# A fused layer on Trainium2: SyncE's DMA queue, in place of GpSimd's, copies q into its stacks

## Chip, cores and metric

One Trainium2 chip, one core of it. The metric is the device time of one execution in microseconds, smaller is better.

## What is computed

The reference is one transformer layer on four sequences (B = 4) of 512 rows and 512 columns, all in float32. Cut to its core:

```python
q = rotary(heads(x @ Wq + bq))        # 16 heads of 32
k = rotary(x @ Wk + bk)               # one key head, one value head
v = x @ Wv + bv
attn = softmax(q @ k.T / sqrt(32))
x = layernorm(x + (attn @ v) @ Wo + bo)
h = sigmoid(x @ quant(w1).T) * (x @ quant(w2).T)   # 1408 wide, weights in -1, 0, 1
x = layernorm(x + h @ quant(w3).T)
```

## The kernel before, in words

The program is written out by hand: each engine has its own list of instructions, and semaphores tie the lists together. The four sequences are called b = 0 to 3 here, as in the code.

**Attention in steps.** From b = 1 on, a sequence is 32 steps, k = 0 to 31. Step k takes head h = k // 2 and its pair i = k % 2: two of the four blocks of 128 query rows. In each step TensorE multiplies the stacked q with the stacked k (`score`, line 1355), VectorE takes the row minimum (`row_max`, line 1046), ScalarE takes two exponentials (`exps`, line 752) and the upper f16 half of p (`p_high`, line 760), VectorE takes the lower half (`p_low`, line 1053), and one DMA transpose on SyncE's queue (`turn`, line 477) turns p into `pt_sb`. The step with number k turns the pair k - 1. Four heads later `context` (line 1413) multiplies the turned p with v, for four heads at once; it stands in TensorE's list at steps 12, 20 and 29 and, for the last four heads, at step 2 of the next sequence. The table `BESIDE` says what else TensorE does in each step: projections of q and k, and all of the feed-forward part of the sequence before. `exps` waits until the pair four earlier is turned, since p has four slots. So `turn` has about three steps to land, except for the last pair of a sequence, which the context at step 2 wants.

**How q comes to its stack.** For a group g of four heads, ScalarE adds the bias (`unit`), GpSimd and VectorE rotate (`rotation`, lines 532 to 540, and `pairs`, line 925), ScalarE copies the result to `hi`, rounded for the matmul (`high_half`, line 682), and VectorE puts the rest into `lo` (`halves`, line 956). `hi` and `lo` are one buffer each of 128 rows (four heads of 32 rows). `stack(engine, b, h)` (lines 421 to 432) then issues four DMAs of 64 KB that put the rows of head h of `hi` and `lo` on the 128 partitions of one of four slots of `q_st`, so that one matmul adds up the products of the halves. It waits until the slot's last head (four before) is scored, until `hi` is written and, ahead of its third DMA, until `lo` is. Who waits for a stack: `score` of that head in step 2h, and `high_half` of the next group (steps 2, 10, 18 and 26 of ScalarE's list), since it writes over `hi`.

**The queues.** For b = 0 SyncE's queue issues the stacks. For b = 1 to 3 GpSimd's list does, in between its rotations, `inverse_std` (lines 561 to 568, for the layer norms), `add_bias` (line 573) and the rounding of weights. SyncE's list for b = 1 to 3 is the 96 `turn`s, with the loads of xT (line 459, at step 7, for the next sequence) and of x (line 463, at the end of step 12), and the stores of finished rows (line 470, at steps 1, 2, 3 and 5). Each list goes on in order: what stands behind a wait waits too. `q_slot` gives the slot and the semaphore of a head; before, the stacks of SyncE and those of GpSimd count on separate semaphores (`q_in` and `q_by_pool`).

Of the kernel before, what the change touches and what calls it, by code (L numbers as in the profile page):

```python
# [31 lines left out]
B, T, D, H, F = 4, 512, 512, 16, 1408  # L32
# [4 lines left out]
HPG = H // HG  # L37
# [17 lines left out]
QR = 4  # L55
SUMS = 4
PIECES = 4
FIRST_RING = 4
WARM = 10
UNITS = ["q0", "k", "q1", "q2", "q3"]  # L60

# [140 lines left out]
def unit_count(s, name):  # L202

    return s * len(UNITS) + UNITS.index(name)


def layer(nc, xT, x, wq, small, wo, b_rows, w1, w2, w3, table, out):
    with ExitStack() as ctx:
# [3 lines left out]
        def sem(name):  # L212
            return ctx.enter_context(nc.semaphore(name))
# [112 lines left out]
        hi_done = sem("hi_done")  # L326
        lo_done = sem("lo_done")
        q_in = [sem(f"q_in{n}") for n in range(QR)]
        q_by_pool = [sem(f"q_by_pool{n}") for n in range(QR)]
        scored = sem("scored")  # L330
        maxed = sem("maxed")
        expd = sem("expd")
# [34 lines left out]
        def filled(use, s, n=0):  # L367

            name = banks_of(use, s)[n]
            return wide[name][1], at(name, use, s)  # L370
# [28 lines left out]
        def h_of(s):  # L399


            return h_last if s == B - 1 else h_sb

        def first_bank(n):
            return (score_banks[0:3] + [b_ps[:, :]])[n % FIRST_RING]

# [7 lines left out]
        def q_slot(b, h):  # L414

            n = b * H + h
            if b == 0:
                return n % QR, q_in[n % QR], (n // QR + 1) * 16 * 4
            return n % QR, q_by_pool[n % QR], ((n - H) // QR + 1) * 16 * 4

        def stack(engine, b, h):

            n, name = b * H + h, f"q{h // HPG}"
            slot, stacked, _ = q_slot(b, h)
            if n >= QR:
                engine.wait_ge(scored, (n - QR + 1) * TT)
            engine.wait_ge(hi_done, unit_count(b, name) + 1)
            for r in (0, 2, 1, 3):
                half = (hi, lo)[r % 2]
                if r == 1:  # L430
                    engine.wait_ge(lo_done, unit_count(b, name) + 1)
                engine.dma_start(q_st[HD * r:HD * (r + 1), slot, :].bitcast(F32),  # L432
                                 half[HD * (h % HPG):HD * (h % HPG + 1), :].bitcast(F32)).then_inc(stacked, 16)
# [18 lines left out]
        @block.sync  # L452
        def _(sp):
            def load_xT(s):
                if s:
                    sp.wait_ge(*filled("q3", s - 1))
                for half in range(2):
                    cols = slice(half * DT * T // 2, (half + 1) * DT * T // 2)
                    sp.dma_start(xT_sb[:, :, :].rearrange("p k t -> p (k t)")[:, cols],
                                 xT[s, :, cols]).then_inc(xT_in[half], 16)  # L460

            def load_x(s):
                sp.dma_start(xb, x[s, :, :].rearrange("(t p) d -> p t d", p=P)).then_inc(x_in, 16)

            def store(s, t):
                if s < B - 1:
                    sp.wait_ge(normed, s * TT + t + 1)
                else:
                    sp.wait_ge(last_normed, t + 1)
                sp.dma_start(out[s, t * P:(t + 1) * P, :], h_of(s)[:, t, :]).then_inc(h_free[t], 16)  # L470

            def turn(b, h, i):

                n = pair_of(b, h, i) % PSLOTS
                sp.wait_ge(p_lo, pair_of(b, h, i) + 1)
                sp.wait_ge(ctx_filled, (b * H + h - PTR) // HPG + 1)
                sp.dma_start_transpose(
                    pt_half[:, (b * H + h) % PTR, i, :, :, :, :].rearrange("p s t k q -> p (s t k) q"),
                    p_half[n][:, :, :].rearrange("p s c -> p (s c)")).then_inc(turned[n], 16)

            load_xT(0)
            sp.wait_ge(xT_in[1], 16)
            sp.dma_start(wq_sb[:, :, P:], wq[:, P:].rearrange("(k p) n -> p k n", p=P)).then_inc(wq_in, 16)
            sp.dma_start(stage[0][:, 0:DT * F // 2], w1[:, 0:DT * F // 2]).then_inc(w_ffn[0], 16)
            for h in range(HPG):
                stack(sp, 0, h)
            sp.dma_start(stage[0][:, DT * F // 2:], w1[:, DT * F // 2:]).then_inc(w1_rest, 16)
            sp.dma_start(stage[1], w2).then_inc(w_ffn[1], 16)
            stack(sp, 0, HPG)
            sp.dma_start(wo_sb[:, :, :], wo.rearrange("(k p) n -> p k n", p=P)).then_inc(wo_in, 16)  # L490
            for h in range(HPG + 1, 3 * HPG):
                stack(sp, 0, h)
            load_xT(1)
            for h in range(3 * HPG, H):
                stack(sp, 0, h)
            sp.wait_ge(rounded, 2 * PIECES)
            load_x(0)
            sp.dma_start(stage[2], w3).then_inc(w_ffn[2], 16)
            for t in range(TT):
                sp.sem_inc(h_free[t], 16)  # L500
            for b in range(1, B):
                for k in range(H * PAIRS):
                    if k == 7 and b < B - 1:
                        load_xT(b + 1)
                    if k:
                        turn(b, *divmod(k - 1, PAIRS))
                    elif b > 1:
                        turn(b - 1, H - 1, 1)
                    if b > 1 and k in (1, 2, 3, 5):
                        store(b - 2, (1, 2, 3, 5).index(k))  # L510
                    if k == 12:
                        sp.wait_ge(h_ready, b * TT)
                        load_x(b)
            turn(B - 1, H - 1, 1)
            for t in range(TT):
                store(B - 2, t)
            for t in range(TT):
                store(B - 1, t)
            for t in range(TT):
                sp.wait_ge(h_free[t], (B + 1) * 16)  # L520

        @block.gpsimd
        def _(pool):
# [64 lines left out]
                round_weight(1, c)  # L588
            rotation(1, "q0")
            cosines(1, "k")  # L590
            stack(pool, 1, 0)
            add_bias(0, 0)
            add_bias(0, 1)
            sines(1, "k")
            add_bias(0, 2)
            add_bias(0, 3)
            for h in range(1, HPG - 1):
                stack(pool, 1, h)
            for b in range(1, B):
                stack(pool, b, 3)  # L600
                if b > 1:
                    inverse_std(b - 2, 1, 2)
                rotation(b, "q1")
                if b > 1:
                    inverse_std(b - 2, 1, 3)
                stack(pool, b, 4)
                stack(pool, b, 5)
                rotation(b, "q2")
                stack(pool, b, 6)
                inverse_std(b - 1, 0, 0)  # L610
                inverse_std(b - 1, 0, 1)
                if b == 1:
                    pool.wait_ge(thr_step, 2 * 3)
                    round_weight(2, 0, 0)
                stack(pool, b, 7)
                inverse_std(b - 1, 0, 2)
                inverse_std(b - 1, 0, 3)
                if b == 1:
                    round_weight(2, 2, 1)
                stack(pool, b, 8)  # L620
                stack(pool, b, 9)
                rotation(b, "q3")
                if b == 1:
                    stack(pool, b, 10)
                    stack(pool, b, 11)
                    round_weight(2, 1, 2)
                    round_weight(2, 3, 3)
                add_bias(b, 0)
                if b > 1:
                    stack(pool, b, 10)  # L630
                add_bias(b, 1)
                if b > 1:
                    stack(pool, b, 11)
                add_bias(b, 2)
                add_bias(b, 3)
                for h in range(12, H):
                    stack(pool, b, h)
                if b < B - 1:
                    rotation(b + 1, "q0")
                if b < B - 1:  # L640
                    inverse_std(b - 1, 1, 0)
                    stack(pool, b + 1, 0)
                    stack(pool, b + 1, 1)
                    inverse_std(b - 1, 1, 1)
                    rotation(b + 1, "k")
                    stack(pool, b + 1, 2)
            for norm in NORMS[NORMS.index((B - 2, 1, 0)):]:
                inverse_std(*norm)

# [575 lines left out]
        def _(pe):  # L1225
# [102 lines left out]
            def first_score(h, t):  # L1328
                n = h * TT + t
                pe.wait_ge(expd, max(n - FIRST_RING + 1, 0))  # L1330
                if n == FIRST_RING - 1:
                    pe.wait_ge(*unit_drained(0, "k"))
# [211 lines left out]
            pe.wait_ge(ones_set, 1)  # L1544
            for _ in range(WARM):
                pe.matmul(score_banks[0][:, 0:P], ones[:, :], ones[:, :], start=True, stop=True)
# [88 lines left out]
```

## Time and profile before

| | us |
|---|---|
| median of 3 runs | 600.63 (598.98 to 602.34) |
| the profiled execution | 601.29 |
| its span in the trace | 599.4 |
| TensorE busy in the span | 546.4 (91%) |
| VectorE busy | 476.7 (80%) |
| ScalarE busy | 420.6 (70%) |
| GpSimd busy | 299.7 (50%) |

Durations below are from the profiled execution; all times of the trace are counted from the start of its span. In its rows PE is TensorE's matmul, DVE VectorE, ACT ScalarE, POOL GpSimd and SP SyncE; "SPq" and "POOLq" are their instruction queues, which issue DMAs. The duration of a DMA row on SPq or POOL is the time in which the queue issues it; the time to landing is given apart, from the start of the issue until the data is there. "x96" is a count, "<-" in brackets names what ended an idle time, and L432 is line 432.

### The profile page before, as it was taken

The numbers are of one execution on the slowest core, as the hardware profiler recorded it, in microseconds if no ns is written. First come the engines' busy times: TensorE is split into PE (matmuls) and PEld (weight loads), VectorE is DVE, ScalarE is ACT, GpSimd is POOL, SyncE is SP. The second block draws the span as 40 slices with busy tenths as digits, with TensorE's granted clock in tenths as the row PEclk, the third lists the DMA queues.
The fourth block names the chain that finished last, engine by engine and source line by source line (L and its number), as shares of the span: only waits on it lengthen the run. The fifth ranks groups of instructions, "written<-read, shape, count | busy, mean of one in ns | idle before, by whom it ended". The sixth has DMA issues, their size and how long they took to land.

```text
span 599.4 us, 9184 instructions
## 1 busy us (share of the span) xinstructions
PE 546.4 (91%) x2984; PEld 274.5 (46%) x2984; DVE 476.7 (80%) x639; ACT 420.6 (70%) x857; POOL 299.7 (50%) x398
## 2 busy tenths in 40 slices
PE   9788889898788999999799999999699999989993
PEld 5454445544444444454444445355244444444441
DVE  3788978978998999889989899889989897445433
ACT  2657757779787988787898888678979896233300
POOL 2209796928897734868357335896553300211011
PEclk9779999999979999999999999999799999999997
DMA  8680418239989997999999988989999989000001
GB/s 311 187 310 10 132 41 293 71 65 181 212 147 210 167 181 145 176 193 203 214 199 192 187 163 154 181 187 184 175 217 177 170 177 190 37 0 37 1 0 70
DMA packets 217119, 92.12 MB, mean 154 GB/s; under 512 B 204400, under 2 KB 205552, under 8 KB 216560
## 3 DMA queue, kind: packets, MB, share of 16 engines
q1 hardware_dynamic: 209952, 77.61, 63.9%
q0 software_dynamic: 6144, 12.60, 10.2%
q10 hardware_dynamic: 976, 1.33, 0.6%
q8 instruction: 24, 0.39, 0.3%
q14 instruction: 23, 0.19, 0.1%
HBM read 20.20 MB, written 4.19 MB: 41 GB/s over the span
## 4 chain that ended last, share of the span: by engine, by line
PE 62%; DVE 13%; issue 8%; ACT 8%; DMA 5%; POOL 2%; SPq 1%; ACTq 0%; POOLq 0%; DVEq 0%
PE a_ps L1310 12%; PE b_ps L1310 7%; PE c_ps L1413 7%; PE s_ps L1323 6%; PE s_ps L1355 5%; PE e_ps L1310 5%; DVE p_all L1053 3%; PE b_ps L1323 3%; PE a_ps L1241 3%; DMA pt_sb<-p_all 3%; PE c_ps L1395 3%; ACT p_all L752 2%; PE a_ps L1323 2%; DVE sh_sb L1046 2%; PE s_ps L1366 2%
## 5 line engine op out<-in xcount | busy, mean ns | idle before, releaser
L752 ACT ACTIVATE p_all<-s_ps,sh_sb 128x512 f32<-128x512 f32 x192 | 129.9, 682 | 58.5 <-DVE sh_sb L1046 55.5
L1053 DVE SCALAR_TENSOR_TENSOR p_all<-p_all 128x1024 f16<-128x1024 f32 x96 | 128.6, 1340 | 4.6 <-ACT p_all L760 4.5
L1046 DVE TENSOR_REDUCE sh_sb<-s_ps 128x2 f32<-128x1024 f32 x96 | 116.6, 1215 | 17.2 <-PE s_ps L1355 17.2
L760 ACT ACTIVATE p_all<-p_all 128x1024 f16<-128x1024 f32 x96 | 101.7, 1059 | 2.0
L1310 PE MATMUL a_ps<-late,q 128*128 128x512 f16 x352 | 83.5, 380 | 4.6 <-ACT th L723 2.9
L1355 PE MATMUL s_ps<-k_st,q_st 128*128 128x512 f32 x192 | 79.5, 496 | 2.8 <-ACT p_all L752 1.6
L432 POOL DMA_DIRECT2D q_st<-hi x96 | 49.4, 517 | 59.3 <-PE s_ps L1355 31.4
L561 POOL TENSOR_SCALAR rstd<-mv 128x1 f32<-128x1 f32 x32 | 9.9, 308 | 132.9 <-DVE mv L1013 132.8
L1310 PEld LDWEIGHTS a_ps<-late,q 128*128 128x128 fp8e4 x352 | 31.9, 98 | 47.1 <-issue 7.5
L739 ACT ACTIVATE p_all<-s_ps,sh_sb 128x512 f32<-128x512 f32 x48 | 32.9, 689 | 27.9 <-DVE sh_sb L1040 27.8
L432 POOL DMA_DIRECT2D q_st<-lo x96 | 47.2, 497 | 7.0 <-DVE lo L956 6.7
L1413 PE MATMUL c_ps<-pt_sb,vh 128*32 128x512 f16 x768 | 46.9, 400 | 0.6 <-DMA pt_sb<-p_all 0.5
L1355 PEld LDWEIGHTS s_ps<-k_st,q_st 128*128 128x128 f32 x192 | 34.5, 193 | 26.7 <-issue 15.8
L532 POOL TENSOR_TENSOR rot<-raw,table_sb 128x512 f32<-128x512 f32 x20 | 26.3, 1317 | 39.1 <-ACT raw L673 33.2
L1310 PE MATMUL b_ps<-late,q 128*128 128x512 f16 x192 | 45.4, 379 | 0.0
L537 POOL TENSOR_TENSOR rot<-rot,table_sb 128x512 f32<-128x512 f32 x18 | 23.9, 1328 | 30.8 <-DVE rot L925 30.5
L1310 PE MATMUL e_ps<-late,q 128*128 128x512 f16 x160 | 37.8, 379 | 0.0
L752 ACT ACTIVATION_READ_ACCUMULATOR p_all<-s_ps,sh_sb 128x1 f32 x192 | 37.8, 197 | 0.0
L1241 PE MATMUL a_ps<-xT_sb,wq_sb 128*128 128x512 f32 x72 | 35.6, 611 | 0.8 <-ACT rT L784 0.7
L1040 DVE TENSOR_REDUCE sh_sb<-s_ps 128x1 f32<-128x512 f32 x48 | 31.3, 680 | 3.9 <-PE s_ps L1338 3.8
L1323 PE MATMUL s_ps<-q,late 128*128 128x512 fp8e4 x154 | 34.1, 379 | 0.0
L1413 PEld LDWEIGHTS c_ps<-pt_sb,vh 128*32 128x32 f16 x768 | 20.5, 101 | 24.5 <-issue 8.0
(160 smaller groups left out, 1012.0 us busy)
## 6 DMA issues: line engine op xcount, KB each, us to landing
q_st<-hi POOLq DMA_DIRECT2D x96, 64.0 KB, 3.5
q_st<-lo POOLq DMA_DIRECT2D x96, 64.0 KB, 4.3
late<-in_w SPq DMA_DIRECT2D x2, 2816.0 KB, 14.1
xT_sb<-in_xT SPq DMA_DIRECT2D x8, 512.0 KB, 5.4
late<-in_x SPq DMA_DIRECT2D x4, 1024.0 KB, 6.5
out<-late SPq DMA_DIRECT2D x12, 256.0 KB, 2.9
late<-in_w SPq DMA_DIRECT2D x2, 1408.0 KB, 7.1
q_st<-hi SPq DMA_DIRECT2D x32, 64.0 KB, 2.0
```

Source lines behind the costliest of these rows:

```text
L432: engine.dma_start(q_st[HD * r:HD * (r + 1), slot, :].bitcast(F32), half[HD * (h % HPG):HD * (h % HPG + 1), :].bitcast(F32)).then_inc(stac ...
L739: act.activation(p_sb[:, h % 2, t, :], first_bank(n), ACT.Exp, bias=sh_sb[:, n % (2 * PSLOTS):n % (2 * PSLOTS) + 1], scale=-1.0, accum_out ...
L752: act.activation(p_pair[n][:, t % 2, :], pair_banks(h * PAIRS + t // 2)[:, t % 2, :], ACT.Exp, bias=sh_sb[:, 2 * n + t % 2:2 * n + t % 2 + ...
L760: act.activation(p_half[n][:, 0, :], p_pair[n].rearrange("p t k -> p (t k)"), ACT.Copy, scale=P_SCALE).then_inc(p_hi, 1)
L1040: dve.tensor_reduce(sh_sb[:, n % (2 * PSLOTS):n % (2 * PSLOTS) + 1], first_bank(n), AX.X, ALU.min).then_inc(maxed, 1)
L1046: dve.tensor_reduce(sh_sb[:, 2 * n:2 * n + 2], pair_banks(h * PAIRS + i), AX.X, ALU.min).then_inc(maxed, 2)
L1053: dve.scalar_tensor_tensor(out=p_half[n][:, 1, :], in0=p_pair[n].rearrange("p t k -> p (t k)"), scalar=P_SCALE, in1=p_half[n][:, 0, :], op ...
L1241: mm = pe.matmul(ps[:, :], wq_sb[:, k, g * P:(g + 1) * P], xT_sb[:, k, :], start=(k == 0), stop=(k == DT - 1))
L1310: mm = pe.matmul(ps[:, :], w[:, k, f * P:(f + 1) * P], hT[:, n, k, :], start=(k == 0 and n == 0), stop=(k == DT - 1 and n == 1))
L1323: mm = pe.matmul(ps[:, :], gT[:, n, f, t * P:(t + 1) * P], q3v[:, f, :], start=(f == 0 and n == 0), stop=(f == FT - 1 and n == 1))
L1355: pe.matmul(pair_banks(n)[:, t % 2, :], q_st[:, slot, t * P:(t + 1) * P], k_st[:, b % 2, :], start=True, stop=True).then_inc(scored, 1)
L1413: mm = pe.matmul(c_ps[HD * j:HD * (j + 1), :], vh[:, m, k, :], pt_half[:, (b * H + g * HPG + j) % PTR, :, n, :, k, :], start=(k == 0 and n ...
```

## The change

SyncE's list now has the stacks of b = 1 to 3, GpSimd's has none. A table says ahead of which step's `turn` each stack stands. Its entries (s, h) are head h of the sequence b + s. So head 3 of a sequence comes at step 1, heads 4 and 5 at step 5, head 6 at step 7 (behind the load of xT), head 7 at step 9, heads 8 and 9 at step 13, 10 at 14, 11 at 16, 12 at 20, 13 at 21, 14 at 22, 15 at 24, and heads 0, 1 and 2 of the next sequence at 28, 28 and 30. Heads 0 to 2 of b = 1 stand ahead of all steps. Both sets of stacks now count on `q_in`.

```diff
+STACKS = {1: [(0, 3)], 5: [(0, 4), (0, 5)], 7: [(0, 6)], 9: [(0, 7)], 13: [(0, 8), (0, 9)], 14: [(0, 10)],
+          16: [(0, 11)], 20: [(0, 12)], 21: [(0, 13)], 22: [(0, 14)], 24: [(0, 15)], 28: [(1, 0), (1, 1)], 30: [(1, 2)]}
...
-        q_by_pool = [sem(f"q_by_pool{n}") for n in range(QR)]
...
             n = b * H + h
-            if b == 0:
-                return n % QR, q_in[n % QR], (n // QR + 1) * 16 * 4
-            return n % QR, q_by_pool[n % QR], ((n - H) // QR + 1) * 16 * 4
+            return n % QR, q_in[n % QR], (n // QR + 1) * 16 * 4
...
+            for h in range(HPG - 1):
+                stack(sp, 1, h)
             for b in range(1, B):
                 for k in range(H * PAIRS):
                     if k == 7 and b < B - 1:
                         load_xT(b + 1)
+                    for s, h in STACKS.get(k, []):
+                        if b + s < B:
+                            stack(sp, b + s, h)
                     if k:
                         turn(b, *divmod(k - 1, PAIRS))
```

In GpSimd's list all calls `stack(pool, ...)` go, 48 of them, and the rest stays in its order:

```diff
             cosines(1, "k")
-            stack(pool, 1, 0)
             add_bias(0, 0)
...
             for b in range(1, B):
-                stack(pool, b, 3)
                 if b > 1:
                     inverse_std(b - 2, 1, 2)
                 rotation(b, "q1")
                 if b > 1:
                     inverse_std(b - 2, 1, 3)
-                stack(pool, b, 4)
-                stack(pool, b, 5)
                 rotation(b, "q2")
-                stack(pool, b, 6)
                 inverse_std(b - 1, 0, 0)
```

## Rows read from the trace of the kernel before

**Rows 1.** Busy us of each engine by sequence, granted clock, DMA share

```profile
117.00:252.00 135.00, 125.53 (x677) 60.19 (x675) 119.58 (x147) 113.01 (x225) 89.90 (x115) 0.97 0.89 164
...
382.00:506.00 124.00, 116.52 (x659) 57.36 (x660) 110.81 (x137) 103.94 (x208) 55.88 (x86) 0.97 1.01 185
```

**Rows 2.** The same columns for five us of the second sequence

```profile
165.00:170.00 5.00, 3.42 (x22) 2.02 (x26) 5.00 (x5) 4.97 (x11) 4.83 (x4) 0.62 0.57 111
```

**Rows 3.** The page's part 4, the chain that ended last by engine

```profile
PE 62%; DVE 13%; issue 8%; ACT 8%; DMA 5%; POOL 2%; SPq 1%; ACTq 0%; POOLq 0%; DVEq 0%
```

**Rows 4.** The chain around 186 and 255: start, us, what

```profile
178.86 12.23 DMA pt_sb<-p_all
...
255.36 5.10 DMA pt_sb<-p_all
```

**Rows 5.** ACT and PE timelines there: start, us, instruction, idle before

```profile
191.18 0.69 ACT L752 ACTIVATE p_all<-s_ps,sh_sb 128x512 f32<-128x512 f32 x1 [2.64 <-DMA pt_sb<-p_all]
...
193.17 0.60 PE L1310 MATMUL a_ps<-late,q 128*128 128x512 f16 x2 [1.68 <-ACT th L723]
...
260.59 0.61 PE L1413 MATMUL c_ps<-pt_sb,vh 128*32 128x512 f16 x8 [0.53 <-DMA pt_sb<-p_all]
```

**Rows 6.** Waits (us, times, longest), and the stack instructions by engine

```profile
POOL rstd L561 <- DVE mv L1013: 132.8, 30, 38.3
...
ACT p_all L752 <- DMA pt_sb<-p_all: 2.6, 1, 2.6
...
PE c_ps L1413 <- DMA pt_sb<-p_all: 0.5, 1, 0.5
...
L432 POOL DMA_DIRECT2D q_st<-hi x96: 496/496/737, 102.5 to 476.7; - x96
...
L432 SPq DMA_DIRECT2D q_st<-hi x32: 507/588/632, 13.5 to 91.5; - x32
```

**Rows 7.** The page's part 6: DMA issues, KB each, median us to landing

```profile
q_st<-lo POOLq DMA_DIRECT2D x96, 64.0 KB, 4.3
...
out<-late SPq DMA_DIRECT2D x12, 256.0 KB, 2.9
...
q_st<-hi SPq DMA_DIRECT2D x32, 64.0 KB, 2.0
```

**Rows 8.** L477, last eight turnings: ns min/median/max, and landing

```profile
L477 SPq DMA_TRANSPOSE pt_sb<-p_all x8: 1317/1958/2875, 486.3 to 505.6; - x8
...
DMA to landing us min/median/max: 4.3/4.5/4.7
```

**Rows 9.** L477, steps 4 to 8, each sequence; one turning; landing of xT

```profile
L477 SPq DMA_TRANSPOSE pt_sb<-p_all x5: 2089/3173/4432, 139.1 to 157.1; - x5
...
L477 SPq DMA_TRANSPOSE pt_sb<-p_all x5: 2748/3727/5492, 272.2 to 290.9; - x5
...
L477 SPq DMA_TRANSPOSE pt_sb<-p_all x5: 2453/3692/5285, 401.8 to 417.9; - x5
...
285.29 5.49 SPq L477 DMA_TRANSPOSE pt_sb<-p_all  x1
...
DMA to landing us min/median/max: 5.4/5.9/6.4
```

**Rows 10.** Timeline of ACT: copies into hi: q1, q2 (b=2), q2 (b=3)

```profile
264.67 0.62 ACT L682 ACTIVATE hi<-rot 128x512 fp32r<-128x512 f32 x1
...
298.07 0.61 ACT L682 ACTIVATE hi<-rot 128x512 fp32r<-128x512 f32 x1
...
427.74 0.61 ACT L682 ACTIVATE hi<-rot 128x512 fp32r<-128x512 f32 x1
```

**Rows 11.** For b=1: load of x (SP timeline, landing) and PE step 16

```profile
177.37 0.57 SPq L463 DMA_DIRECT2D late<-in_x  x1
...
DMA to landing us min/median/max: 7.7/7.7/7.7
...
186.74 0.58 PE L1355 MATMUL s_ps<-k_st,q_st 128*128 128x512 f32 x1
```

More of the change, by code:

```diff
@@ L596, in _ @@
             add_bias(0, 3)
-            for h in range(1, HPG - 1):
-                stack(pool, 1, h)
             for b in range(1, B):
-                stack(pool, b, 3)
                 if b > 1:
@@ L614, in _ @@
                     round_weight(2, 0, 0)
-                stack(pool, b, 7)
                 inverse_std(b - 1, 0, 2)
@@ L619, in _ @@
                     round_weight(2, 2, 1)
-                stack(pool, b, 8)
-                stack(pool, b, 9)
                 rotation(b, "q3")
                 if b == 1:
-                    stack(pool, b, 10)
-                    stack(pool, b, 11)
                     round_weight(2, 1, 2)
@@ L628, in _ @@
                 add_bias(b, 0)
-                if b > 1:
-                    stack(pool, b, 10)
                 add_bias(b, 1)
-                if b > 1:
-                    stack(pool, b, 11)
                 add_bias(b, 2)
                 add_bias(b, 3)
-                for h in range(12, H):
-                    stack(pool, b, h)
                 if b < B - 1:
@@ L641, in _ @@
                     inverse_std(b - 1, 1, 0)
-                    stack(pool, b + 1, 0)
-                    stack(pool, b + 1, 1)
                     inverse_std(b - 1, 1, 1)
                     rotation(b + 1, "k")
-                    stack(pool, b + 1, 2)
             for norm in NORMS[NORMS.index((B - 2, 1, 0)):]:
```

## The prediction, written before the changed kernel ran

> **What bounds the kernel now.** I read the busy time by sequence first. TensorE is busy for 125.5 of 135 us while b = 1 runs (93%) and 116.5 of 124 us (94%) in b = 3 [rows 1]. It sets the pace; VectorE and ScalarE have 10 to 20% to spare, GpSimd a third to a half. So I look for what TensorE still waits for. One part is its clock: the granted clock averages 0.97 in either sequence [rows 1], since it falls to the 1.2 GHz level for a few microseconds, at 165 to 170 for example, where TensorE had been idle in part; its mean there is 0.62 [rows 2]. The other part is in the chain of work that ended last: DMA 5%, GpSimd 2% [rows 3]. In its order of time, the turning of p stands in it twice only: once with 12.23 us at 178.86, once with 5.10 us at 255.36 [rows 4]. Behind the first, ScalarE stood still for 2.64 us until 191.18, and through it TensorE for 1.68; behind the second, TensorE waited 0.53 us itself [rows 5]. These two are also all that anyone waited for a turned p in b = 1 to 3 (the two waits on a DMA in [rows 6]). No one waited for a stack of q: the lists of waits have no such row. And GpSimd waits for others rather than they for it: 132.8 us for VectorE's statistics alone [rows 6].
>
> **What goes from GpSimd.** 48 stacks of four DMAs, 192 issues of 0.50 us [rows 6]: 96 us. GpSimd isn't the pace and isn't waited for, so this is worth nothing at the end. What hides it is its own waiting; only norms or rotations that stood behind a stack start earlier, and their users (ScalarE's rows of h, its copies into `hi`) come at fixed places of a list that wasn't late for them.
>
> **What comes to SyncE.** The same 192 issues at 0.59 us [rows 6]: 2.36 us a stack, 113 us in all. A turning takes SyncE 1.96 us in the last eight, with no stack about, and lands in 4.5 [rows 8]; in steps 4 to 8, with GpSimd's stacks and the loads on the same DMA engines, it takes 3.2, 3.7 and 3.7 by the medians [rows 9]. Per sequence of some 130 us that gives SyncE 32 x 1.96 + 16 x 2.36 = 100 us if the stacks no longer slow the turnings, or, with 3.5 as the mean of those three, 32 x 3.5 + 38 = 150 us, more than there is, if they do. This is the unknown of the change. I take the low value at the start of a busy stretch: the extra time came from transfers that ran beside the turnings, and now the queue issues a stack after a turning, whose issue then has room. Loads stay slow: the turning behind xT took 5.49 [rows 9], and I keep that.
>
> *Steps 5 to 9 of b = 2*, four stacks close together, are the tightest. From the turning at 272.2 [rows 9]: three turnings 5.9, stacks 4 and 5 4.7, a store 0.6, the xT load 1.1, stack 6 2.4, which gives 286.9; the turning behind xT 5.5, the next 2.0, stack 7 2.4: 296.7. Its last DMA is issued 0.6 us earlier and lands 2.0 us after that issue if it is as when SyncE's stacks ran alone, 2.9 as the stores do behind turnings, 4.3 as the slower half of GpSimd's [rows 7]. That is 298.1, 299.0 or 300.4. ScalarE writes over `hi` at 298.07 [rows 10] and must have all four stacks landed. So it stands still for 0 to 2.3 us; I take 0.9, the stores being nearest in queue and neighbours. It falls into the part where TensorE waits for ScalarE's rows of h, so I count it in full: +0.9. In b = 3 no xT is loaded: the last of the five turnings starts at 417.9 [rows 9], and 417.9 + 2.0 + 2.4 + 2.3 = 424.6 against 427.74 [rows 10]: hidden by 3 us. Head 3 at step 1: 255.36 + 2.0 + 2.4 + 2.3 = 262.0 against 264.67 [rows 4, 10]: hidden by 2.6.
>
> *The first turning of the chain.* After the load of x at 177.37 [rows 11] stacks 8 and 9 are now issued ahead of the turning: it starts 177.9 + 4.7 = 182.7, not at 178.86. The load lands 7.7 us after its issue, at 185.1 [rows 11]; the turning should land at 182.7 + 4.5 = 187.2 or, if its data only starts then, at 189.6. ScalarE was ready at 191.18 - 2.64 = 188.54. Before, GpSimd's DMAs ran beside this turning; that is what I think made 12.23 of it. Bounds: it lands in time (-1.7, all of TensorE's idle time), or it takes 12.23 again from its later start (+3.8). The nearest rows, the landing of the load and of an undisturbed turning, say the first: -1.7.
>
> *The second.* Stacks 2 and 3 were issued beside it and now aren't: it lands in 4.5 in place of 5.10, so the 0.53 goes: -0.5; at worst 0. What is late next there is VectorE's p, no DMA.
>
> *Heads 0 to 2 of b = 1* now stand ahead of SyncE's step 1, where the queue has nothing else; they go out no later than before: 0. The other stacks of a sequence have over a step to spare: 0. The turnings that come 2.4 or 4.7 us later have about three steps of 4 us until `exps`; except for the xT place, 0.
>
> **Sum.** -1.7 - 0.5 + 0.9 = -1.3 us against the profiled execution's 601.29: 600.0. That execution was 0.66 above the median of the runs, so by the median I expect 600.63 - 1.3 = 599.3.
>
> **A rule against the change.** The rows show that a stack from GpSimd's queue and a turning overlapped, at the price of 4.3 us to landing where SyncE's stacks, alone, needed 2.0 [rows 7]. *The Trainium skill, "DMA: Bandwidth & Descriptors", sections "SWDGE vs HWDGE vs iDMA" and "Queues, rings and completion order": each DMA engine takes turns between the internal queues that software- and hardware-made descriptors feed, while inside one ring descriptors are taken in order. By that a stack could pass a megabyte load before, and can't now.* No row of before shows the new order, so it is a rival.
>
> **The rivals.**
>
> *Ring order bites (0.08, 602.1).* Stack 8 sits behind the load of x. It would land at 185.1 + 2.3 = 187.4, and TensorE scores it at 186.74 [rows 11]: 0.7 us idle, in b = 1 and again in b = 2; and the copy into `hi` waits 2.3 in place of 0.9: 599.3 + 1.4 + 1.4. For it: both sit close to the edge. Against: the load starts earlier if the turning ahead of it is shorter. This is the page's rule at work.
>
> *SyncE's queue is full, slower (0.20, 608).* The turnings stay as slow as they were, because the engines are still shared with loads and stacks. Then in b = 2: 272.2 + 5 x 3.7 + 4 x 2.36 + 1.7 = 301.8, the last DMA landed 1.4 later at the least, 303.2: ScalarE waits 5.1 us at 298.07. In b = 3: 401.8 + 18.5 + 9.4 + 0.6 + 1.4 = 431.7 against 427.74: 4.0. In b = 1: 139.1 + 15.9 + 9.4 + 1.5 + 1.4 = 167.3, where the same copy has its place: about 0. Together 9.1 in place of 0.9: 599.3 + 8.2 = 607.5, some 608 with the idle time of the queue. It decides from a mean turning of about 2.9 us in these steps; half way to it gives 603. For it: all three medians of rows 9 are over that. Against: rows 8.
>
> *A fall of the clock goes, faster (0.22, 595.3).* In b = 1 and b = 3 it costs 3% of 135 and of 124 us, 4 us each [rows 1]. It came behind idle stretches in steps 9 to 12, where TensorE waits for rows of h; GpSimd's stack 7 stood ahead of two of the norms there. If these come sooner, or VectorE's work shifts a little, one fall may go: 599.3 - 4.0. Against: GpSimd was waiting for VectorE's statistics, not late. The same thing can go the other way in b = 2, whose mean I haven't counted on.
>
> *None of this.* That the change doesn't do what it says can be excluded but for this: the 12.23 us may be the load's work, which stays. That is in the main case.
>
> **Chances.** The main case has 0.50: a queue that fits, 597 to 602. What a measurement of this kernel can tell from no change is about 0.5%, 3.0 us: 597.6 to 603.6. Of the 0.50, 0.07 lies below, 0.39 inside, 0.04 above (the +3.8 of the first turning). With the clock's 0.22 below, the ring order's 0.08 inside and the full queue's 0.20 above: faster 0.29, same 0.47, slower 0.24. The range goes from 594.8, just past the clock's case, to 606.5, which takes in half of the full queue's (it has a mild form) and leaves out about 0.1 there and 0.05 below.
>
> **What will show it.** Right: turnings of about 2 us on SyncE's queue in steps 4 to 8, SyncE's stacks landing in 2 to 3 us, no ScalarE wait of 2.6 us on `pt_sb` near 190, no TensorE wait on `pt_sb` at step 2 of b = 2, and a wait of under 1.5 us ahead of line 682 near 298. Wrong: waits of ScalarE on `q_st` of several us ahead of line 682 at step 10; turnings that start 5 us and more behind VectorE's p_low for many steps; a TensorE wait on `q_st` at step 16; another number of falls of the granted clock.

## The result: 0.4% slower, and the profile after

The changed kernel takes 602.83 us, the kernel before 600.56 in the same comparison: a ratio of 1.0042 with a 95% interval of 1.0021 to 1.0062, slower by 2.3 us by the medians and 2.5 by the ratio. The prediction said 599.3, faster by 0.2%, and gave 597.6 to 603.6 (no change that can be told) a chance of 0.47. The size is inside its range; the sign is not the forecast one.

The profiled execution took 604.24 us with a span of 602.4 (before: 601.29 and 599.4). Its page begins:

```profile
span 602.4 us, 9184 instructions
...
PE 547.1 (91%) x2984; PEld 275.6 (46%) x2984; DVE 478.1 (79%) x639; ACT 420.8 (70%) x857; POOL 208.3 (35%) x206
...
PE 53%; DVE 18%; issue 9%; ACT 8%; DMA 8%; SPq 2%; POOL 0%; POOLq 0%; ACTq 0%; DVEq 0%
PE a_ps L1294 9%; DMA pt_sb<-p_all 7%; PE c_ps L1397 6%; PE b_ps L1294 5%; DVE p_all L1037 5%; PE s_ps L1307 5%; PE s_ps L1339 4%; PE e_ps L1294 4%; DVE sh_sb L1030 3%; PE a_ps L1307 3%; ACT p_all L736 3%; PE a_ps L1225 3%; PE c_ps L1379 2%; SPq L432 2%; PE s_ps L1350 2%
```

GpSimd lost 91 us of work, as expected, and it left the chain of work that ended last (2% before, [rows 3]). What came in its place is the row below it: the turning of p (DMA pt_sb<-p_all) is 7% of the chain, 42 us, where it stood in it twice with 17.3 us [rows 4], and SyncE's issue of stacks (SPq L432) is in it with 2%. The lists of waits name who waits for a DMA (us, times, longest):

```profile
ACT p_all L736 <- DMA pt_sb<-p_all: 9.4, 8, 2.2
PE c_ps L1397 <- DMA pt_sb<-p_all: 4.3, 3, 2.0
ACT hi L666 <- DMA q_st<-lo: 1.0, 1, 1.0
```

ScalarE and TensorE wait 13.7 us for turned p where it was 3.1 [rows 6]. How late the turnings are can be read from the start of each of the 96 and the end of the `p_low` that it waits for: 82 start more than 1 us behind their p, 48 more than 3 us, 13 more than 5 us, and the latest 7.9 us. Before, these were 15, 4 and none, and the latest 4.2 us. From its start a turning lands no later than before (median 4.6 us, before 5.0); it is the start that is late.

**How a turning comes to be late.** SyncE's queue in steps 26 to 31 of b = 1 and at the start of b = 2 (start, us, instruction, count; a row of several turnings spans the waits between them):

```profile
237.88 1.17 SPq L432 DMA_DIRECT2D q_st<-hi  x2
239.11 1.22 SPq L432 DMA_DIRECT2D q_st<-lo  x2
240.42 1.17 SPq L432 DMA_DIRECT2D q_st<-hi  x2
241.63 1.22 SPq L432 DMA_DIRECT2D q_st<-lo  x2
242.95 5.05 SPq L477 DMA_TRANSPOSE pt_sb<-p_all  x2
248.09 1.48 SPq L432 DMA_DIRECT2D q_st<-hi  x2
249.62 1.22 SPq L432 DMA_DIRECT2D q_st<-lo  x2
250.94 6.63 SPq L477 DMA_TRANSPOSE pt_sb<-p_all  x3
```

Three stacks take 4.8 and 2.7 us, and from 237.88 to 257.57 the list has no pause over 0.2 us: it runs behind. The turning at 250.94 has its p from this instruction of VectorE, which ended at 245.94, five microseconds earlier:

```profile
244.01 1.93 DVE L1037 SCALAR_TENSOR_TENSOR p_all<-p_all 128x1024 f16<-128x1024 f32 x1
```

The last turning of b = 1, the one that TensorE waits for at step 2, is the third of that row. In the chain, then in TensorE's timeline:

```profile
254.17 1.30 SPq L477
...
255.56 5.01 DMA pt_sb<-p_all
```

```profile
260.71 1.48 PE L1397 MATMUL c_ps<-pt_sb,vh 128*32 128x512 f16 x24 [1.82 <-DMA pt_sb<-p_all]
```

Its p was there at 254.17, 1.2 us earlier than before, but SyncE was still issuing the turning ahead of it (1.30 us of SPq in the chain). So it started at 255.56, 0.2 us later than in [rows 4], landed no sooner, and the 1.2 us that had been won were lost in the longer wait: 1.82 us against 0.53 [rows 5]. At the same place of b = 3 the wait is 1.97 us, at 392.17, and it was nothing before. (What this wait cost beyond its own length is told below.) Where the stack of head 15 stands ahead of a turning of b = 3, ScalarE's exponentials four pairs later feel it:

```profile
484.65 1.21 DVE L1037 SCALAR_TENSOR_TENSOR p_all<-p_all 128x1024 f16<-128x1024 f32 x1
```

```profile
492.37 4.44 DMA pt_sb<-p_all
```

```profile
496.89 0.69 ACT L736 ACTIVATE p_all<-s_ps,sh_sb 128x512 f32<-128x512 f32 x1 [2.20 <-DMA pt_sb<-p_all]
```

p was ready at 485.86; its turning started 6.5 us later.

**What was won at the same time.** GpSimd's closing drain, an instruction of the program's end that every engine waits for, before and after (line, queue, ns, start):

```profile
L208 POOLq DRAIN  x1: 6891/6891/6891, 592.3 to 592.3; - x1
```

```profile
L211 POOLq DRAIN  x1: 664/664/664, 598.7 to 598.7; - x1
```

Its start stands 2.2 us behind TensorE's last matmul in either kernel, so it marks the end of the computation: 598.7 against 592.3, and the steps lost 6.4 us, not 2.5. (This is one execution against one. The changed kernel's is 1.4 us above its median, the other's 0.7, so by the medians the steps lost 5.7.) Before, the drain then ran until 599.2, 3.4 us past SyncE's own last work at 595.8. After, it hides behind the last store. 6.4 - 3.4 = 3.0 is the difference of the two spans.

**The granted clock.** Its mean over the span was 0.972 and is 0.973, and that hides a difference, since part of the low time before lies at the start or behind TensorE's last matmul. Between 40 and 585 us TensorE was at the 1.2 GHz level for 13.7 us before, in two stretches, and for 20.5 us after, in four. One of the new ones stands right behind the wait of 1.97 us at step 2 of b = 3. The rows are before and after in turn (start and end, length, busy us of PE, PEld, DVE, ACT and POOL, clock, DMA share), then TensorE's context there, before and after:

```profile
40.00:585.00 545.00, 508.94 (x2845) 252.35 (x2844) 448.12 (x593) 402.06 (x816) 290.75 (x383) 0.99 0.76 147
40.00:585.00 545.00, 503.56 (x2810) 250.36 (x2809) 445.84 (x586) 402.27 (x817) 197.64 (x187) 0.98 0.71 147
392.00:396.00 4.00, 4.00 (x42) 1.99 (x35) 3.93 (x6) 3.57 (x8) 3.24 (x5) 1.00 0.95 214
392.00:396.00 4.00, 3.83 (x40) 1.85 (x44) 2.53 (x4) 3.39 (x6) 3.21 (x4) 0.57 0.77 157
```

```profile
390.26 3.64 PE L1413 MATMUL c_ps<-pt_sb,vh 128*32 128x512 f16 x64
392.17 5.32 PE L1397 MATMUL c_ps<-pt_sb,vh 128*32 128x512 f16 x64 [1.97 <-DMA pt_sb<-p_all]
```

The same 64 matmuls take 1.7 us longer, so this place costs 3.7 us and not 2.0. Two of the kernels below (the sixteenth of the bytes, and GpSimd with heads 0 to 3) wait 2.5 and 2.3 us there, and the clock falls at 392.5 and 392.1; before, there was neither the wait nor the fall.

**Where the 6.4 us come from.** The starts of `p_low`, compared pair by pair, say how far the changed kernel is behind the kernel before (a minus: ahead), so the change from row to row is what the stretch cost or gave:

| at | us behind |
|---|---|
| start of b = 1 | 0.1 |
| step 17 of b = 1 (first turning of the chain) | -1.2 |
| step 2 of b = 2 (wait for the turned p) | 0.1 |
| step 17 of b = 2 (tight place; the clock fell at 296.8) | 1.3 |
| step 31 of b = 2 (GpSimd's rotation of k) | -0.1 |
| step 2 of b = 3 (wait for the turned p, clock) | 3.6 |
| step 30 of b = 3 (`exps` of step 27 and on) | 6.9 |
| mark at the end | 6.4 |

The gain of 1.4 us at the end of b = 2 is GpSimd's. Before, VectorE waited for its rotation of k, and TensorE for VectorE's `k_st`:

```profile
DVE k_st L945 <- POOL rot L540: 1.2, 1, 1.2
PE s_ps L1355 <- DVE k_st L947: 1.2, 1, 1.2
```

All five kernels in which GpSimd issues all 48 stacks have these two waits, and none of the eight in which it issues fewer.

### The profile page after: what moved, and what is told of

Read it like the earlier page. It is cut to its first block, busy times and chain, and to the rows that moved or that the text cites. A ratio compares the mean times of both kernels' runs of the same rounds, so it can differ in the third digit from the quotient of the medians.

```text
span 602.4 us, 9184 instructions
## 1 busy us (share of the span) xinstructions
PE 547.1 (91%) x2984; PEld 275.6 (46%) x2984; DVE 478.1 (79%) x639; ACT 420.8 (70%) x857; POOL 208.3 (35%) x206
## 4 chain that ended last, share of the span: by engine, by line
PE 53%; DVE 18%; issue 9%; ACT 8%; DMA 8%; SPq 2%; POOL 0%; POOLq 0%; ACTq 0%; DVEq 0%
PE a_ps L1294 9%; DMA pt_sb<-p_all 7%; PE c_ps L1397 6%; PE b_ps L1294 5%; DVE p_all L1037 5%; PE s_ps L1307 5%; PE s_ps L1339 4%; PE e_ps L1294 4%; DVE sh_sb L1030 3%; PE a_ps L1307 3%; ACT p_all L736 3%; PE a_ps L1225 3%; PE c_ps L1379 2%; SPq L432 2%; PE s_ps L1350 2%
## 5 line engine op out<-in xcount | busy, mean ns | idle before, releaser
L566 POOL TENSOR_SCALAR rstd<-mv 128x1 f32<-128x1 f32 x32 | 8.3, 260 | 192.8 <-DVE mv L997 192.8
L537 POOL TENSOR_TENSOR rot<-raw,table_sb 128x512 f32<-128x512 f32 x20 | 29.0, 1451 | 64.7 <-ACT raw L657 58.9
L578 POOL TENSOR_TENSOR late<-late,b_sb 128x512 f32<-128x512 f32 x16 | 25.4, 1613 | 20.9 <-DMA late<-in_x 20.9
L986 DVE SCALAR_TENSOR_TENSOR b_ps<-th,b_ps 128x512 f32<-128x512 f32 x24 | 16.7, 694 | 19.7 <-PE b_ps L1294 16.2
```

Source lines behind the costliest of these rows:

```text
L537: pool.tensor_tensor(rot[:, 0, :], raw[:, n % 2, :], cos_sb, ALU.mult).then_inc(cos_done, 1)
```

## The experiments

Theory A: each stack costs SyncE's list 2.4 us of issue ahead of a turning; where stacks stand close, the list falls behind. Theory B: the stacks' bytes slow the turnings in SyncE's queue. Theory C: GpSimd's own work, come free, disturbs VectorE.

### SyncE issues heads 8 to 11 only

```diff
+BY_SP = [8, 9, 10, 11]
...
                     for s, h in STACKS.get(k, []):
-                        if b + s < B:
+                        if b + s < B and h in BY_SP:
                             stack(sp, b + s, h)
```

(GpSimd's list has the stacks of the other heads where it had them, on a semaphore of its own.)

> SyncE issues heads 8 to 11 of b = 1 to 3 only, at the places of the change; GpSimd keeps the other 36 stacks. Theory A (each stack costs SyncE's list 2.4 us of issue ahead of a turning, the list runs 3 to 8 us behind p, and turnings that are waited for land late): the loss at step 2 of the next sequence and near step 27 goes, the gain of b = 1 at step 16 stays: 599.4, ratio 0.996 to 1.000. Theory B (the stacks' data in the turnings' own ring slows them): about a quarter of the loss stays: 601. Theory C (GpSimd's own work, come free, disturbs VectorE): between the two kernels, 601 to 602.

Measured: 596.5 us, ratio 0.9918 (0.9892 to 0.9944), faster than both kernels and by more than expected. Waits on a turned p:

```profile
ACT p_all L766 <- DMA pt_sb<-p_all: 2.0, 1, 2.0
...
PE c_ps L1427 <- DMA pt_sb<-p_all: 1.0, 2, 0.7
```

```profile
L211 POOLq DRAIN  x1: 2971/2971/2971, 591.6 to 591.6; - x1
```

The steps end at 591.6 on this mark, 0.7 before the kernel before. The rest, 3.4 us, is the drain: 3.0 us behind GpSimd's 144 DMAs, hidden behind the last store. B's quarter of the loss isn't there. Of theory C this kernel says little, since GpSimd keeps 36 of the 48 stacks; the kernel with two DMAs a stack decides it below.

### GpSimd keeps heads 0 to 3

```diff
+BY_SP = [4, 5, 6, 7, 8, 9, 10, 11, 12, 13, 14, 15]
```

> As the changed kernel, but GpSimd keeps heads 0 to 3 of every sequence (the stacks of steps 28, 30 and 1). Theory A: the turnings of steps 28 to 31 start with p again, so TensorE's wait on the turned p at step 2 falls from 1.8 and 2.0 us to 0.5 or less, and with it 2 to 3 us of the time: 600.5, ratio 0.998 to 1.002; the ScalarE waits near step 27 of b = 3 stay. Theory B: the wait at step 2 stays near its size before, 0.5, but nothing more is gained. Theory C: 602.5, as the changed kernel, for the norms and rotations are as free as there.

Measured: ratio 1.0030 (1.0006 to 1.0055). This was a miss: the ratio is above the forecast. The first wait at step 2 was gone as expected, but the second wasn't:

```profile
PE c_ps L1427 <- DMA pt_sb<-p_all: 3.0, 2, 2.3
```

At the end of b = 2 SyncE still had a backlog from steps 20 to 24, and GpSimd's two stacks now ran beside the late turnings (its rows begin at 378.79; SyncE's four turnings from 375.36 on took 14.32 us without a pause). So the places where heads 0 to 3 stand aren't the whole of it; the load on the list over a sequence is. The steps end at 598.2 by the mark, no sooner than those of the changed kernel once both are counted from their first turning (126.4 here, 127.4 there), and GpSimd's drain, 4.6 us behind 48 DMAs, ends 1.1 us after SyncE's last work at 601.7. The ratios differ by 0.0012 with intervals of 0.002 on either, so a small gain in the steps is neither shown nor excluded.

### The same issues with a sixteenth of the bytes

This kernel leaves out 480 of the 512 columns of each stack of b = 1 to 3.

```diff
+                cols = slice(0, T if b == 0 else T // 16)
-                engine.dma_start(q_st[HD * r:HD * (r + 1), slot, :].bitcast(F32),
-                                 half[HD * (h % HPG):HD * (h % HPG + 1), :].bitcast(F32)).then_inc(stacked, 16)
+                engine.dma_start(q_st[HD * r:HD * (r + 1), slot, cols].bitcast(F32),
+                                 half[HD * (h % HPG):HD * (h % HPG + 1), cols].bitcast(F32)).then_inc(stacked, 16)
```

> The changed kernel with every stack DMA of b = 1 to 3 cut to 32 of its 512 columns: the same 192 issues in the same places, one sixteenth of the bytes (scores of b = 1 to 3 are then made from what lay in the slots). Theory A: nothing changes, turnings still start 3 to 7 us behind p in the same steps: 602 to 603.5, ratio 1.002 to 1.006. Theory B: the time of before or less, 599 to 600.5, ratio under 1.000.

Measured: ratio 1.0007 (0.9984 to 1.0029), between the two forecasts. TensorE's waits for turned p are as in the changed kernel, ScalarE's are smaller:

```profile
PE c_ps L1398 <- DMA pt_sb<-p_all: 4.3, 3, 2.5
ACT p_all L737 <- DMA pt_sb<-p_all: 2.3, 3, 1.0
```

```profile
L211 POOLq DRAIN  x1: 669/669/669, 596.7 to 596.7; - x1
```

By the mark the steps still lose 4.4 of the 6.4 us (596.7 against 592.3). An issue takes as long as in the changed kernel (0.59 us), and 42 turnings still start more than 3 us late. So with one sixteenth of the bytes two thirds of the loss remain, and the bytes explain some 2 us; the two ratios differ by 0.0035 with intervals of 0.002 on either, so this share is known to a factor of two at best.

### The kernel before, with small copies in SyncE's list

```diff
+            def small_copies(n):
+                for r in range(4):
+                    c = n
+                    sp.dma_start(spare[HD * r:HD * (r + 1), c:c + 1], ones[0:HD, 0:1]).then_inc(spared, 16)
...
+                    for s, h in STACKS.get(k, []):
+                        if b + s < B:
+                            small_copies(count)
+                            count += 1
```

> The kernel before, with GpSimd's stacks as they were, and 192 tiny copies (32 numbers each) in SyncE's list at the places where the changed kernel has its stacks; they wait for nothing and nobody needs them. Theory A: the time of the changed kernel or more, since the turnings are slowed by GpSimd's stacks too: 603 to 607, ratio 1.004 to 1.011. Theories B and C: 600.5, ratio 0.998 to 1.002.

(It issues 180 copies, not 192: the three stacks ahead of b = 1 have none.) Measured: ratio 1.0719 (1.0676 to 1.0762), some 43 us slower, six times and more what was expected.

```profile
ACT p_all L767 <- DMA pt_sb<-p_all: 62.8, 32, 4.6
PE c_ps L1428 <- DMA pt_sb<-p_all: 9.9, 3, 4.7
```

The direction is A's: copies of 32 numbers each, which nobody waits for, make ScalarE wait 32 times, and 76 of the 96 turnings start more than 3 us behind their p. The size isn't explained in full. A turning takes longer to issue beside GpSimd's stacks (median 2.58 us here, 2.35 in the changed kernel), so the list is full in most steps; and TensorE was at the 1.2 GHz level for 34 us between 40 and 585 us, where it had been 13.7. How the 43 us divide between the two I haven't worked out.

### Two DMAs of each stack in place of four

This kernel leaves out the second copies of `hi` and `lo` in b = 1 to 3.

```diff
-            for r in (0, 2, 1, 3):
+            for r in (0, 2, 1, 3) if b == 0 else (0, 1):
```

> The changed kernel with two of the four DMAs of each stack of b = 1 to 3 left out (the second copies of hi and lo, so these two blocks of a slot keep what lay there): 1.2 us of issue a stack in place of 2.4, half the bytes. Theory A (time of issue ahead of the turnings): turnings start at most 1 to 2 us behind p where they started 3 to 8 behind, the waits of TensorE and ScalarE on the turned p fall from 13.7 us to under 4, TensorE ends 4 to 7 us earlier than in the changed kernel: 596.5 to 599, ratio 0.991 to 0.997. Theory B (bytes): a sixteenth of the bytes gave some 2 us, so half of them gives 1: 601.8.

Measured: 595.27 us, ratio 0.9895 (0.9872 to 0.9917), better than theory A had said. No wait on a turned p is left in its lists at all, only 12 turnings of 96 start more than 1 us behind their p, and the latest 2.6 us.

```profile
L211 POOLq DRAIN  x1: 664/664/664, 589.8 to 589.8; - x1
```

Half the issues win 8.9 us of steps over the changed kernel (589.8 against 598.7), and still 6.9 over the kernel with a sixteenth of the bytes and all the issues. This decides between A and B: it is the time of issue, with a small share for the bytes. Nor is it that more DMAs are in flight: from its start a turning lands in 4.4 us here and in 4.6 in the changed kernel (medians), and what fell is the time from p to that start. It decides on C too: GpSimd has no stack here either, and nothing is lost. The clock isn't the difference by itself: TensorE was at the 1.2 GHz level for 20.6 us between 40 and 585 us, as in the changed kernel, but not at step 2 of b = 3. The kernel also says what the move could have given with a stack that is cheap to issue: steps that end 2.5 us sooner than before, and the drain on top.

### The closing drain: more DMAs by GpSimd

These two are the kernel before, with tiny DMAs of GpSimd's that nobody needs, in the last feed-forward part:

```diff
+                if norm == (B - 1, 1, 0):
+                    for n in range(44):
+                        r, c = n % 4, n // 4
+                        pool.dma_start(spare[HD * r:HD * (r + 1), c:c + 1], ones[0:HD, 0:1]).then_inc(spared, 16)
```

> The kernel before with 44 tiny DMAs more from GpSimd (32 numbers each), in the last feed-forward part, where it waits 38 us for VectorE: 236 in all. On GpSimd's closing drain, which took 6.9 us behind 192 DMAs, 3.0 behind 144, 4.6 behind 48 and 0.7 behind none. Theory D (the drain clears what is left since a last clearing, every 116 DMAs, at 0.082 us each: 76, 28, 48 and 0 left): 4 left, a drain of 1.0 us, hidden behind the last store: 597.2, ratio 0.993 to 0.996. Rival E (the drain grows with all DMAs since the start, the others being chance): 8 us or more: 601.5 to 602.

> The same with 24 tiny DMAs, 216 in all. Theory D: 100 left, a drain of 8.9 us, 2.0 us longer than before and none of it hidden: 602.6, ratio 1.002 to 1.005. Rival E: 7.5 us, 601.1.

Measured: ratio 1.0070 (1.0051 to 1.0088) with 44, 1.0041 (1.0022 to 1.0060) with 24. The drains were 10.48 us and 8.85 us.

```profile
L208 POOLq DRAIN  x1: 10484/10484/10484, 592.2 to 592.2; - x1
```

For 216 DMAs theory D had 8.9; for 236 it had 1.0, and failed. Rival E's "8 us or more" is met with 236, but its 7.5 us with 216 is not. Each DMA more costs 0.082 us of drain (3.59 us for 44), but nothing is cleared at each 116th. The drain is a cost by itself, as both kernels run their steps as before (the mark stands at 592.2 with 44).

### Sixty more

> The kernel before with 60 tiny DMAs more from GpSimd at the same place, 252 in all. Closing drains so far: 6.89 us behind 192, 8.85 behind 216, 10.48 behind 236, 2.97 behind 144, 4.60 behind 48: 0.66 + 0.082 for each DMA left, with 116 fewer left than issued once more than 128 were; the 129th of the kernel before came 3.02 us late for no wait. Theory D2 (a ring of 128: when it is full, all but 12 are cleared): the next clearing comes at the 245th, 20 are left, the drain takes 2.3 us and hides behind the last store: 597.3, ratio 0.993 to 0.996. Theory F (only one clearing ever, 0.082 us a DMA after it): 136 left, 11.8 us: 605.5 to 607.

Measured: ratio 0.9999 (0.9981 to 1.0017), a drain of 6.57 us behind 252 DMAs. Neither forecast: shorter than behind 236, so there is a second clearing, but with some 72 left ((6.57 - 0.66) / 0.082), not 20.

### Heads 8 to 13 for SyncE

```diff
-STACKS = {..., 13: [(0, 8), (0, 9)], 14: [(0, 10)], 16: [(0, 11)], 20: [(0, 12)], 21: [(0, 13)], 22: [(0, 14)], ...}
+STACKS = {..., 12: [(0, 8)], 13: [(0, 9)], 15: [(0, 10)], 16: [(0, 11)], 20: [(0, 12)], 22: [(0, 13)], ...}
+BY_SP = [8, 9, 10, 11, 12, 13]
```

> SyncE issues heads 8 to 13, the last two at steps 20 and 22, GpSimd the other 30 stacks (120 DMAs: none cleared before the end, since the ring isn't full: 120 left by theory D2, a drain of 10.5 us, 7 of it behind the last store: ratio 0.999 to 1.003). If the ring is cleared at 116 and not at 128, 4 are left and the ratio is 0.990. In the steps, theory A: turnings of steps 20 to 24 up to 2.5 us behind p, no wait on them: TensorE ends as with heads 8 to 11, at 588 to 589.

Measured: ratio 1.0018 (0.9999 to 1.0036), with 120 DMAs of GpSimd's:

```profile
L211 POOLq DRAIN  x1: 10484/10484/10484, 592.1 to 592.1; - x1
```

A drain of 10.5 us, as forecast for a ring that hadn't been cleared, against 3.0 behind 132 and 144. Twelve DMAs fewer cost 7.5 us of drain, and 7.1 of its 10.5 us stand behind SyncE's last work at 595.5. The steps end at 592.1 by the mark, TensorE's work 2.2 us before it at 589.8, about 1 us later than the forecast and 0.5 us later than with heads 8 to 11.

### Heads 8 to 11 spread, and heads 7 to 11

```diff
-STACKS = {..., 13: [(0, 8), (0, 9)], 14: [(0, 10)], 16: [(0, 11)], ...}
+STACKS = {..., 12: [(0, 8)], 13: [(0, 9)], 15: [(0, 10)], 16: [(0, 11)], ...}
```

> As the version in which SyncE issues heads 8 to 11 only, these now at steps 12, 13, 15 and 16 in place of 13, 13, 14 and 16, so no step has two. Theory A: turnings of steps 13 to 15 start 2 to 3 us behind p in place of 4 to 6, the 1 us lost at step 13 of b = 2 and 0.7 at step 12 of b = 3 come back: TensorE ends 1 us earlier, ratio 0.988 to 0.992. If it gives nothing (0.992 again), these losses are the load of x alone.

> SyncE issues heads 7 to 11, spread over steps 9, 12, 13, 15 and 16, GpSimd the other 33 stacks (132 DMAs, a drain of 2.0 us, hidden). Theory A: one more stack for SyncE at step 9 makes the turnings of steps 9 to 12 2 us late, within what their users can bear; the turning behind xT in b = 2 no longer has GpSimd's stack beside it: ratio 0.988 to 0.993, no worse than with heads 8 to 11. If step 10's exponentials then wait for a turning, 0.994.

Measured: 0.9927 (0.9908 to 0.9946) and 0.9919 (0.9892 to 0.9946), neither to be told from the 0.9918 of heads 8 to 11. So spreading the stacks gave nothing that can be told, and the first forecast (0.988 to 0.992) was missed. The marks of the profiled executions are a microsecond earlier, 590.6 and 590.3 against 591.6, but so are their first turnings, at 126.2 and 126.6 against 127.3, where the lists don't differ yet; most of that microsecond isn't from the change.

## Why the prediction was right and where it failed

**Right: the tight place.** "So it stands still for 0 to 2.3 us; I take 0.9": 1.0 us was measured, ahead of line 666 in b = 2, and none elsewhere. That it agrees to 0.1 us is luck in part: the turning behind xT took 3.1 us in place of 5.49, the pauses and the other turnings made the list end 1 us later all the same, and the last DMA landed 2.06 us after its issue in place of 2.9.

**Right in these steps: prices.** Five turnings of steps 4 to 8 of b = 2 took 2.1 us by the median, where they had taken 3.7 [rows 9] and the prediction took 2.0 except behind xT:

```profile
L477 SPq DMA_TRANSPOSE pt_sb<-p_all x5: 1709/2102/3097, 272.3 to 292.7; - x5
```

```profile
q_st<-hi SPq DMA_DIRECT2D x128, 64.0 KB, 2.0
```

Stacks landed in 2.0 us. The rival of the full queue needed a mean of 2.9 us a turning; here the mean was 2.35. But its direction was the right one: over a whole sequence the turnings had a mean of 2.3 to 2.5 us and not 1.96, and SyncE's list, with its loads and stores, issued for 115, 121 and 112 us in b = 1, 2 and 3, of 130, 129 and 122 us. The prediction had 100 for turnings and stacks.

The ring-order rival didn't come: TensorE never waited for a stack. The load of x was issued at 175.94 and landed at 182.33, and stack 8 behind it took 4.3 to 5.3 us to land, where others take 2.0; it was there at 183.2, and TensorE scored it at 186.44. *That is as the rule of the Trainium skill has it ("DMA: Bandwidth & Descriptors", "Queues, rings and completion order", on descriptors that are taken in order inside a ring).* It cost nothing, as the load landed 2.8 us earlier than in the rival's sum.

**About right: the first turning.** -1.7 was forecast for b = 1; the lead was 1.2 us from step 17 on, as two idle pieces of TensorE, 0.46 and 0.31 us, were left where there had been one of 1.68. The turning landed in 4.6 us in place of 12.23.

**Wrong: "The turnings that come 2.4 or 4.7 us later have about three steps of 4 us until `exps`; except for the xT place, 0."** This is the step that failed. It priced each late turning alone. A step with a stack takes SyncE some 2.3 + 2.4 = 4.7 us and a step is 4 us long; from step 20 to 24 four of five steps have one, from 28 to 30 there are three stacks, from 5 to 9 four. The delay is carried on, to 3 to 8 us, and meets users with less slack than three steps: the exponentials of step 27 (2.20 us at once), and the context at step 2. I had worked out the mean load, 100 of 130 us, and one burst, for one user, and left out the same sum for the other bursts and for the turnings themselves. In its place the runs showed a list that falls behind and waits of 13.7 us for turned p, all gone with half the issues. The steps lost 6.4 us where the sum had -1.3, so 7.7 us were left out; about 2 of them are the bytes, and 1.7 the low clock behind the wait of step 2 of b = 3.

**Wrong: "it lands in 4.5 in place of 5.10, so the 0.53 goes: -0.5; at worst 0."** It landed in 5.01, behind a turning that was itself late, and the wait there grew to 1.82 us (and to 1.97 at the same step of b = 3). The bound had the wrong side closed: moving a stack away from a place leaves its backlog there.

**Wrong: "GpSimd isn't the pace and isn't waited for, so this is worth nothing at the end."** GpSimd was waited for at two places that the change touched. Its rotation of k came late at the end of b = 2, which cost TensorE 1.2 us, and the change gave 1.4 there; the lists of waits of the kernel before had both lines. And its drain ended 3.4 us after everything else, which is gone now. For the drain, the difference between the last store's landing and the end of the span would have shown it: SyncE had its last work done at 595.8, and the span ended at 599.4.

**The clock.** The prediction gave a chance to a fall that goes and said that b = 2 could go the other way; that way it went, in b = 2 and in b = 3.

Of its signs of being right four came (turnings of about 2 us in steps 4 to 8, stacks in 2 us, no wait near 190, a short one near 298), and the one on TensorE's wait at step 2 of b = 2 failed. Of its signs of being wrong two came: turnings that start over 5 us behind p, 13 of 96, and another number of falls of the clock. The two profiled executions differ by +3.0 us and the sum had -1.3. The error of 4.3 is the 7.7 us that the steps lost beyond the sum, less the 3.4 of the drain. So that the time still lay near 600 is luck: two things that the prediction hadn't seen went against each other.

*The Trainium skill, "DMA: Bandwidth & Descriptors", section "Issuing engines are not separate DMA queues", calls the sequencer's time to start a DMA usually small beside the DMA itself. The trace doesn't agree for these transfers of 64 KB:* each takes 0.59 us to issue and lands 2.0 us after the start of its issue, and four of them hold up the list for 2.4 us.

## What to carry to other kernels

A queue in which each entry waits for data has a budget per step, not only a mean: add up the issue time of all that stands in a step, carry what is over to the next step, and compare the running sum with the slack of whoever waits for the entries that are pushed back. An unloaded engine's queue isn't free to give away either: look at how the program ends, and who is the last to finish there. A wait of the engine that sets the pace can cost more than its length, if its clock falls behind it: look at the granted clock by stretches, not at its mean. And a part of a change can be worth more than the whole: a quarter of the stacks, moved alone, gave 0.8%, of which the profile puts 0.7 us on the steps and 3.4 on a shorter drain.

## What the runs showed of the hardware that I hadn't expected

GpSimd's closing drain depends on how many DMAs it has issued, by steps that aren't monotone: 0.66 us behind none, 4.60 behind 48, 10.48 behind 120, 2.97 behind 132 and 144, 6.89 behind 192, 8.85 behind 216, 10.48 behind 236, 6.57 behind 252. Between clearings it grows by 0.082 us a DMA (192 to 236; 48 and 120 fit the same slope from 0.66). In the kernel before, the 129th came after an idle time that no wait explains, and so it did, with 3.0 us, in all four others in which GpSimd issues 48 stacks:

```profile
369.93 0.59 POOL L432 DMA_DIRECT2D q_st<-hi  x1 [3.02 <-issue]
```

A ring of 128 entries that is cleared when it is full and at the end would fit most of these, and this gap; it is a guess from these figures, and no trace shows such a ring. It doesn't fit 132 and 144 having the same drain, nor the 72 left behind 252; how much a clearing takes away stays open. About 3.5 us of the drain hide behind the last store in this kernel. That is also why the number of GpSimd's DMAs, and not only their place, moved the total: by 4 us with 44 more, and by 7 in the kernel with heads 8 to 13, where the drain of the one with heads 8 to 11 was hidden.
